# A graph and mixture-of-experts kernel on one core: the third stage's layer norm is split after five tiles, and the copy of x to the table of sums is issued one stage later

## The reference, cut to what matters

```python
x = x + _L0_gnn_ref(_layernorm(x), ...)          # mean over neighbours, two matrices
x = x + _L0_ffn_ref(_layernorm(x)[None], ...)[0] # 8 experts, top 2 per token, GELU, hidden 1024
x = x + _L1_gnn_ref(_layernorm(x), W, a, src, dst)   # 8 attention heads over the edges
x = x + _L1_ffn_ref(_layernorm(x)[None], ...)[0] # 16 experts, top 2, ReLU, hidden 512

def _L0_ffn_ref(...):
    ...
    y = jnp.einsum('enh,ehd->end', h, W2) + b2[:, None, :]
    sel = jnp.take_along_axis(y_tok, top_idx[:, :, None], axis=1)
    out = (weights[:, :, None] * sel).sum(axis=1)

def _L1_gnn_ref(x, W, a, src, dst):
    h = jnp.einsum('ni,hio->nho', x, W)
    ...
```

## Time and profile before

| | us |
|---|---|
| median of 3 runs | 2689.09 (2683.56 to 2694.71) |
| the profiled execution | 2688.17 |
| its span in the profile | 2686.4 |
| TensorE busy / granted clock, mean | 2123.7 / 0.875 |
| VectorE, ScalarE, GpSimd busy | 1646.8, 1441.8, 1475.8 |
| route of the first experts ends | 931.8 |
| experts end, heads begin | 1379.3, 1381.0 |
| heads end, the scores of the edges begin | 1437.7, 1438.7 |

### The profile page before, as it was taken

One profiled execution on the slowest core, in us unless ns is written; L12 is line 12 of the kernel. 1 busy time (PEld: TensorE's weight loads), 2 busy tenths in 40 slices (PEclk: granted clock), 3 DMA queues, 4 the chain that ended last, 5 costly groups with the idle time before them and its releaser, 6 DMA issues. The chain is left out here.

```text
span 2686.4 us, 60762 instructions
## 1 busy us (share of the span) xinstructions
PE 2123.7 (79%) x15054; PEld 1737.5 (65%) x15055; DVE 1646.8 (61%) x4178; ACT 1441.8 (54%) x3543; POOL 1475.8 (55%) x1435
## 2 busy tenths in 40 slices
PE   4789976677666599999956888888885888579990
PEld 3666644444444489999945787877773677469990
DVE  7889963333333733333357777777877787843337
ACT  6779943333333434434436666666665878333335
POOL 0000067777777045555546777777753999236650
PEclk9989986766677689999977999999996999789995
DMA  3210036433333722222225878778863887552224
GB/s 114 95 59 20 24 88 199 136 106 105 106 104 105 227 52 36 37 37 35 34 79 164 239 240 243 241 239 243 242 192 131 269 260 227 196 182 70 70 65 147
DMA packets 195211, 366.24 MB, mean 136 GB/s; under 512 B 35100, under 2 KB 86086, under 8 KB 194811
## 3 DMA queue, kind: packets, MB, share of 16 engines
q1 hardware_dynamic: 121939, 208.94, 23.2%
q0 software_dynamic: 59776, 145.56, 21.5%
q10 hardware_dynamic: 13351, 9.99, 1.1%
HBM read 269.11 MB, written 95.27 MB: 136 GB/s over the span
## 5 line engine op out<-in xcount | busy, mean ns | idle before, releaser
L904 POOL DMA_INDIRECT weightsL_w<-y_gnn,all_slot_dst x416 | 396.4, 953 | 284.3 <-issue 282.2
L833 POOL DMA_INDIRECT scores_rows<-h_gnn,all_slot_dst x440 | 425.2, 966 | 141.8 <-issue 133.8
L963 PE MATMUL sum_ps<-weightsL_w 128*128 x880 | 345.6, 546 | 155.7 <-SPq L889 86.1
L963 PEld LDWEIGHTS sum_ps<-weightsL_w 128*128 128x128 f32 x880 | 218.1, 267 | 283.3 <-issue 249.3
L977 DVE TENSOR_TENSOR sums_acc<-sums_acc,sum_ps 128x256 f32 x440 | 185.4, 421 | 316.3 <-PE sum_ps L963 267.7
L1686 ACT ACTIVATE sums_acc<-expertsL_hid_ps,expertsL_b 128x128 f32<-128x128 f32 x704 | 197.7, 372 | 302.0 <-PE expertsL_hid_ps L1635 301.7
L1635 PE MATMUL expertsL_hid_ps<-sums_acc,expertsL_w 128*128 128x128 f32 x2816 | 338.6, 277 | 4.6 <-DVE sums_acc L1706 2.8
L2226 PE MATMUL scores_diff_ps<-all_ident,scores_rows 128*128 128x128 f32 x880 | 293.6, 334 | 51.6 <-DMA scores_rows<-h_gnn,all_slot_dst 41.2
L1635 PEld LDWEIGHTS expertsL_hid_ps<-sums_acc,expertsL_w 128*128 128x128 f32 x2816 | 328.5, 194 | 5.3 <-issue 5.2
L1647 PE MATMUL expertsL_out_ps<-weightsL_w,sums_acc 128*128 x1408 | 323.6, 379 | 0.0
L2228 PE MATMUL scores_diff_ps<-scores_minus,scores_node 128*128 128x128 bf16 x2640 | 303.2, 226 | 0.0
(11 more groups left out here) (471 smaller groups left out, 4234.8 us busy)
## 6 DMA issues: line engine op xcount, KB each, us to landing
saved_gnn<-scores_rows SPq DMA_DIRECT2D x220, 264.0 KB
sum_rows<-saved_gnn SPq DMA_DIRECT2D x220, 264.0 KB, 3.2
weightsL_w<-in_L_ffn_W SPq DMA_DIRECT2D x16, 1024.0 KB, 9.2
weightsL_w<-in_L_ffn_w SPq DMA_DIRECT2D x32, 512.0 KB, 8.6
scores_lanes<-slot_lanes SPq DMA_DIRECT2D x44, 320.0 KB
sort_low_b<-low_lanes SPq DMA_DIRECT2D x32, 416.0 KB, 3.6
scores_rows<-h_gnn,all_slot_dst POOLq DMA_INDIRECT x440
weightsL_w<-y_gnn,all_slot_dst POOLq DMA_INDIRECT x416, 2.8
```

Source lines behind the costliest of these rows:

```text
L833: pool.indirect_dma_start(out=self.rows[:, s, :], out_offset=None, in_=table[:, :], in_offset=bass.IndirectOffsetOnAxis(ap=e["slot_dst"][: ...
L904: pool.indirect_dma_start(out=rows[:, at:at + D], out_offset=None, in_=table[:, :], in_offset=bass.IndirectOffsetOnAxis(ap=e["slot_dst"][: ...
L963: last = nc.tensor.matmul(ps[(PAIRS * turn + s // 2) % len(ps)][:, s % 2 * D:(s % 2 + 1) * D], pick[h][:, s % HALF, :], rows[:, bass.ds(pl ...
```

## The change

The copy of x leaves route for the experts' block: SyncE issues it there behind the bias table, once two transposes are done (`turned`, 2). GpSimd's two gathers that wait for the transposes now stand ahead of the first two `bring_share`, and its wait for `begun` is behind those.

The counting and the norm leave `ToHeads` for the heads' block, in two parts (`EARLY`): tiles 0 to 4, when the first two loads have landed, and tiles 5 to 24. SyncE issues the same six loads as before, but the experts' block ends without waiting for them. ScalarE's and GpSimd's staging waits for the first part's scales (`norm.scaled`, 1); ScalarE takes the second root behind `keep(4)`, waits for the second scales, and only then stages tiles 5 and 7; GpSimd waits for the same ahead of tile 6. TensorE does `multiply(4)` ahead of `turn(5)`.

```diff
-                if again:
-                    sp.wait_ge(joined, NT)
-                    sp.dma_start(rows(r["sums"], 0, 1), x[:, 0:1, :]).then_inc(r["begun"], 16)
-                    sp.dma_start(rows(r["sums"], 1, NT + 1), x[:, :, :]).then_inc(r["begun"], 16)
...
+                if scaled:
+                    sp.wait_ge(turned, 2)
+                    sp.dma_start(rows(r["sums"], 0, 1), x[:, 0:1, :]).then_inc(begun, 16)
+                    sp.dma_start(rows(r["sums"], 1, NT + 1), x[:, :, :]).then_inc(begun, 16)
...
                 for b in range(FEW):
                     bring(b)
+                for b in range(2):
+                    pool.wait_ge(turned, b + 1)
+                    bring(b + FEW)
                 if scaled:
                     pool.wait_ge(indices, 2)
                     pool.wait_ge(r["weights_kept"], 32)
                     for b in range(2):
                         bring_share(b)
-                    pool.wait_ge(r["begun"], 32)
-                for b in range(2):
-                    pool.wait_ge(turned, b + 1)
-                    bring(b + FEW)
+                    pool.wait_ge(begun, 32)
...
-    def vector(self, ve, norm):
-        for n, tiles in enumerate(self.PARTS):
-            ve.wait_ge(self.landed[n], 16)
-            for t in range(tiles.start, tiles.stop):
-                self.nc.vector.bn_stats(norm.stats[:, t, :], self.target[:, t, :])
-        ve.drain()
...
-        self.nc.scalar.activation(self.norm.root[:, 0:1], self.c["ones"][:, 0:1], ACT.Sqrt)
-        act.drain()
-        self.norm.root_of_var(self.nc, act)
+        self.nc.scalar.activation(self.root, self.c["ones"][:, 0:1], ACT.Sqrt)
...
-        self.results.vector(ve, self.norm)
-        self.norm.moments(nc, ve)
-        ve.drain().then_inc(self.end, 1)
...
+    EARLY = (slice(0, G), slice(G, NT))
+    LANDED = (2, len(landed))
...
+                pool.wait_ge(norm.scaled, 1)
                 for t in range(0, NT, 2):
+                    if t == G + 1:
+                        pool.wait_ge(norm.scaled, 2)
...
+                def root(n):
+                    act.wait_ge(norm.var_ready, n + 1)
+                    mine = EARLY[n]
+                    nc.scalar.activation(norm.root[:, mine], norm.var[:, mine], ACT.Sqrt).then_inc(norm.rooted, 1)
+                    act.wait_ge(norm.scaled, n + 1)
+
+                root(0)
                 bring(1)
                 bring(3)
                 copy(0)
                 for t in range(NT):
-                    if t + 1 < NT:
+                    if t + 1 == G:
+                        keep(t)
+                        root(1)
+                        bring(t + 1)
+                        bring(t + 3)
                         copy(t + 1)
-                    keep(t)
-                    if t % 2 and t + RING < NT:
+                    else:
+                        if t + 1 < NT:
+                            copy(t + 1)
+                        keep(t)
+                    if G - 1 < t and t % 2 and t + RING < NT:
...
+                    if t + 1 == G:
+                        multiply(t)
+                        turn(t + 1)
+                        continue
...
+                def moments(n):
+                    mine = EARLY[n]
+                    mean, var, raw, gap, scale, shift = (one[:, mine] for one in (norm.mean, norm.var, norm.raw, norm.gap, norm.scale, norm.shift))
...
+                    nc.vector.tensor_scalar(var, raw, 1e-5, None, ALU.add).then_inc(norm.var_ready, 1)
+                    ve.wait_ge(norm.rooted, n + 1)
+                    nc.vector.reciprocal(scale, norm.root[:, mine])
+                    ve.drain()
+                    nc.vector.scalar_tensor_tensor(shift, mean, -1.0, scale, ALU.mult, ALU.mult).then_inc(norm.scaled, 1)
+                first = 0
+                for n, last in enumerate(LANDED):
+                    for part in range(first, last):
+                        ve.wait_ge(landed[part], 16)
+                        tiles = Results.PARTS[part]
+                        for t in range(tiles.start, tiles.stop):
+                            nc.vector.bn_stats(norm.stats[:, t, :], x[:, t, :])
+                    ve.drain()
+                    moments(n)
```

More of the change, by code:

```diff
@@ L1824, in vector @@
         ve.drain()
[L1827 to L1844 removed]
 class ToHeads:
     def __init__(self, nc, m, c, a, x, acc, r, w, ys_d, h):
[L1851 to L1853 removed]
+        self.nc, self.c, self.a, self.h, self.x, self.sums = nc, c, a, h, x, r["sums"]
+        self.root = acc[:, acc.shape[1] - 1:]
         spare = w["first"][:, NT * TOP * D:]
@@ L1866, in load @@
     def load(self, sp):
-        for n in range(len(self.results.PARTS)):
-            self.results.load(sp, n)
+        for n, tiles in enumerate(Results.PARTS):
+            sp.dma_start(self.x[:, tiles, :], rows(self.sums, 1 + tiles.start, 1 + tiles.stop)).then_inc(self.h["landed"][n], 16)
     def tensor(self, pe, bank):
@@ L1992, in heads @@
     RING = 4
-    w, norm = h["w"], h["norm"]
+    w, landed = h["w"], h["landed"]
+    EARLY = (slice(0, G), slice(G, NT))
+    LANDED = (2, len(landed))
     SIZES = (G, G, G, G, 3, 2)
@@ L2591, in build @@
             h = dict(w=acc[:, 0:KD * WIDTH].rearrange("p (k o) -> p k o", k=KD), ends=acc[:, KD * WIDTH:KD * WIDTH + 3 * D].rearrange("p (j d) -> p j d", d=D),
-                     coef=s.sb("coef", [P, 2, KD]), ident=c["ident"][:, :])
+                     coef=s.sb("coef", [P, 2, KD]), ident=c["ident"][:, :], home=acc[:, NT * HROW - HOME:],
+                     landed=[s.sem(f"x_landed{n}") for n in range(len(Results.PARTS))])
             feed_forward(nc, LAYERS[0], c, e, a, x, acc, dram, out, h,
```

32 lines of the change are left out of this document (16 added, 16 removed).

## The result

The kernel after takes 2675.37 us in the median of six runs (2672.17 to 2679.81), the kernel before on the same chip 2685.98 (six runs, 2683.56 to 2694.71): a ratio of 0.9965, with a 95% interval of 0.9952 to 0.9979. The profiled execution took 2679.81 us (before 2688.17).

What follows compares the result with a forecast made beforehand. No engine bounds the kernel throughout; the experts' end runs load, count, norm, barrier. Group 0 gains 6.6 us, 2.6 are given back, the copy 0: 2688.17 less 4.0 is 2684.2, plus 0.9 for the median, 2685; range 2678 to 2692.

Steps and rivals of the forecast that it cites:

- The copy, 0 us: Moving the copy of x from route to the experts gains and loses nothing; it lands at 959.4, before the first scatter.
- the price list: Experts' start: a copy landing after about 968 costs one us per us; at 975 the gain is gone and 3 lost.
- the rival of the late copy: Experts' start: bias table, copy and gathers share transfer engines, so the copy lands late; 2692 us, chance 0.07.
- The block's end: Experts' end waits for SyncE's issuing (1368.37) instead of the norm (1379.30); VectorE starts heads 1.73 us later, at 1370.1.
- the block ends sooner: Rival: the barrier doesn't wait for SyncE's 5.00 us of issuing; heads start 2.3 to 2.5 us earlier, 2682.5, chance 0.13.
- The first norm: Heads' start: five counts 1.7 us, small operations 2.2; scales at 1374.0 instead of staging at 1381.03, 7.0 us earlier.
- Five tiles: Heads: tiles 0 to 4 take 10.2 us instead of 10.7, so tile 4 is kept at 1384.2.
- S: Heads: start of group 0 and of staging tiles 5 to 8, forecast at 1385.1; group 0 began at 1391.73 before.
- GpSimd beside the counting: Heads: VectorE's counts don't hold GpSimd up, so it stages tiles 0, 2 and 4 at 1.22 us each.
- What is given back: Heads: group 1 comes 13.5 us behind group 0 instead of 10.9, so 2.6 of the 6.6 us are lost again.
- the first rival: TensorE's clock falls in the new 3.5 us pause behind tile 4, costing 2 us; 2687, gain 2 us, chance 0.22.
- The sum for heads: Group 1 of heads starts at 1398.6 instead of 1402.59, 4.0 us earlier, and every later block with it.

Runs made afterwards that it cites:

- a scatter at 972: Kernel after with the large copy of x made twice and the experts' first scatter waiting for both; 2676.20 us in one run.
- fewer loads: Kernel after with tiles 5 to 24 of x in one load (2677.33 us), or with early second root and tiles 10 to 24 in one load (2676.30 us).
- the idle transposes: Kernel after with eight transposes into a spare bank on TensorE between tile 4's product and tile 5's transposes; ratio to the kernel before 0.9961.
- the bases: Kernels before and after, each with TensorE's wait numbers in the first aggregation clamped at zero; 2686.03 and 2677.38 us.
- the clears: Kernel before with 1, 2, 8, 17 or 64 small clears on VectorE early in heads; 1 clear 2684.32 us, one run; kernel after with 15, 3024.55 on a slower chip.
- the kernel after with the edit: Kernel after with TensorE's wait numbers in the first aggregation clamped at zero; 2677.38 us, on another chip 2676.39 us.
- e11: Kernel after with ScalarE's second root behind `keep(2)` and tiles 10 to 24 of x in one load, four loads instead of six; 2676.30 us, repeated 2677.48.

## Why the prediction was wrong

**The copy, 0 us: right.** The rows say how near it came. Transfers issued from 900 to 965 us in the kernel after (size, us from issue to landing), answering to the earlier trace rows:

```profile
sums_L<-all_x SPq DMA_DIRECT2D x1, 3200.0 KB, 13.7
...
sums_acc<-in_L_ffn_b SPq DMA_DIRECT2D x1, 1024.0 KB, 5.9
```

Issued at 947.56, the copy takes 13.7 us where 10.1 was assumed, and so lands at 961.3, not 959.4. The first scatter starts at 963.26 (before 962.64), 2 us later, and waits for VectorE still. But the price list was wrong: no us was lost with a scatter at 972, against "from a landing at about 968 on each us costs one". VectorE's third block did start 5 us later there, as the step says; what it left out is that TensorE's work does not wait for it, and that GpSimd makes up some 2 us a block. The landing at 975 that the rival of the late copy names was not run.

**The block's end, 1.73 us behind SyncE's issuing: right** in rule, 1.72 measured. The issuing took 4.07 us instead of 5.00, so the first count came at 1369.29 instead of 1370.1. The rival "the block ends sooner" is refuted by the traces with six loads (1.6 to 1.7 us each time, with the issuing between 4.07 and 5.19); with fewer loads GpSimd's drain is read as the next bound.

**The first norm: right.** Scales at 1372.94, 3.65 us behind the first count, where 3.9 were taken (1374.0 less 1370.1). **Five tiles: right but for 0.2 us**: tile 4 was kept 10.4 us behind the first scales, and S came 0.6 us behind it instead of 0.9.

**GpSimd beside the counting: right.** Three stagings in 3.66 us, as in the kernel before where VectorE did nothing; the Trainium skill, SBUF — State Buffer, Who interferes with whom, has no contention with GpSimd for VectorE's instructions with one SBUF input outside the two-port modes, and the trace agrees.

**What is given back: the number right, partly by luck.** S was 1383.98 for 1385.1, and group 1 at S + 13.56 for S + 13.5. The square came at S + 5.94 (5.9), the rounding was through at S + 9.26 (8.7). But the sum reckons without a lower clock, and the pause was 3.1 us and the clock did fall, as the first rival has it. With the clock kept (the idle transposes) the rounding was through at S + 7.74 and group 1 came at S + 12.68: so the rounding's term was 1.0 us too long and the clock that was left out cost it 1.5 us, and the two nearly cancel. The rival priced the clock at 2 us; it cost 0.85 us at group 1 and 0.1 us at the block's end.

**The sum for heads: 4.0 us forecast, 5.2 measured** from the last scatter to group 1 and 5.5 to the scores (4.7 in the bases). The 1.2 us are the issuing's 0.95, the norm's 0.25 and the root's 0.3, less the tiles' 0.25 and 0.06 of what is given back. Here only sizes were off.

**The step that failed** is the one that closes the sum: "Group 1 starts at 1398.6 instead of 1402.59: 4.0 us earlier, and with it every later block." It takes every later block to keep its length, and gives no reason. The last loop of the third stage runs 4.6 us shorter, since more instructions of VectorE stand ahead of it; the clears show that such a shift alone does it. The prediction lists what the change adds, removes and moves in time, and nothing of it as instructions that shift all that comes behind them. Heads' 5.5 us and the loop's 4.6 make 10.1, where the medians differ by 10.6 in the first comparison and by 8.7 between the bases (there heads gave 4.7). The executions of one kernel lie several us apart, so what is left can't be told.

The forecast of 2685 and the measured 2675.4 lie 9.6 us apart. 4.6 of them are the loop, 1.5 the heads' sizes (5.5 against 4.0), and 3.1 the base: the sum starts from three runs of the kernel before with a median of 2689.09, where six have 2685.98. The loop alone made the difference between about 2680, within the range, and a time below it. And the sentence that the change "is most likely not to be told from none" was wrong: with six runs each the interval of the ratio, 0.9952 to 0.9979, leaves out 1.

## What to carry to other kernels

A loop written once and run many times has a price that can hang on how many instructions stand ahead of it on its engine. Before a gain or loss of less than a per cent is put down to an edit, lay the two traces side by side and look at loops that the edit does not touch; a control with a few idle instructions at a place where the engine waits anyway tells the two apart. And where a loop on the path waits once a turn for a jump back, one or two idle instructions ahead of it are worth a trial: here one was worth 4.6 us in the trace, about as much as the edit's own part in heads. The load of 1.35 us behind the jump, once a turn, is the larger part of that wait, and nothing here was tried on it.

A start that comes sooner is worth what is left of it at the block's end: 0.85 us at group 1 were 0.1 us at the end, and a root 1.5 us sooner, of which 3 us were expected, gave 1.3. And a wait is priced by who runs ahead: where GpSimd's queue can catch up, 10 us cost nothing. A term that comes out right is no proof of its parts: here a rounding reckoned too long hid a clock that was left out, and only the run with the clock kept showed it.

## What the runs showed of the hardware that was not expected

- The jump back of VectorE's loop, up to the load of registers behind it, took 0.51, 0.39 or 0.30 us, by the number of instructions ahead of it; one clear of 128x8 numbers more changed 10.583 us a turn to 10.351.
- The load of the tile numbers into VectorE's registers, once a turn of that loop, took 1.35 us (1.347 to 1.387 in the twenty traces) with the slow and with the fast jump.
- GpSimd's drain at the end of the experts' block took 3.43 us in each of the twenty traces, from about the last scatter's landing on; with three and four loads the first count of heads came 1.5 to 1.6 us behind its end.
- The same six issues of SyncE took 5.19 and 4.59 us in two executions of one program (the kernel after with the edit), and 4.07 in the kernel after.
- The granted clock was still 1.00 in the window of a pause of 3.1 us and 0.57 in the two windows of 2 us behind it, while TensorE was at work again; with eight idle transposes in the pause (1.04 us) it was 1.00 throughout.
- In both profiled executions of e11 the granted clock was 0.50 for 25 us of the fourth stage in which TensorE had no pause; its base had 1.00 there.
- One chip took 13% longer for the whole kernel (3034.7 us), and its heads and its last loop of the third stage took no longer than on the others (10.35 us a turn).
